# Rows of dt and of dt times x, spread for two scan units at a time, in a two-layer decoder with a selective scan

## The reference, cut to what matters

```
dt = softplus(dt_lowrank @ W_dt + b_dt)          # (256 tokens, 512 channels)
dA = exp(dt[..., None] * A)                      # 16 states for each channel
dBx = dt[..., None] * B_t[:, None, :] * x_t[..., None]
h = dA * h + dBx                                 # over the tokens
y_t = sum(h * C_t[:, None, :], axis=-1)
```

## Time and profile before

| what | value |
|---|---|
| time, median of 3 runs | 3942.16 us (3936.2 to 3948.75) |
| the profiled execution | 3951.12 us, span 3949.3 us |
| granted TensorE clock, mean | 0.933 |
| PE, DVE, ACT, POOL busy | 81%, 76%, 49%, 16% |
| DMA queue q1 | 205,552 packets, 467.17 MB, 39.2% of sixteen engines |
| one sequence | 232.8 us |

### The profile page before, as it was taken

The page is one execution under the profiler, slowest core; times in us unless marked ns, Lnnn a source line. Parts: engine busy times, 40 slices in busy tenths (PEclk is TensorE's granted clock), DMA queues, the critical chain, the costliest instruction groups (busy, mean ns, idle before and its releaser), DMA issues.

```text
span 3949.3 us, 57618 instructions
## 1 busy us (share of the span) xinstructions
PE 3210.4 (81%) x21250; PEld 2199.1 (56%) x21250; DVE 3004.6 (76%) x6496; ACT 1953.3 (49%) x4513; POOL 650.5 (16%) x516
## 2 busy tenths in 40 slices
PE   2468988788797888978888897988879888887877
PEld 1245656556464655646556564655646565564655
DVE  5678796877878688796868879687887868778632
ACT  2336455564545546455554645555464554645422
POOL 0303030120303012040210304021030301204000
PEclk8679999999999989999999999989999998999987
DMA  6526171532716235181523517153361614427100
GB/s 213 131 56 174 50 197 63 157 119 89 203 50 184 77 123 153 54 238 49 155 95 116 171 50 225 52 159 99 96 196 50 197 63 146 130 74 215 55 31 16
DMA packets 205833, 470.84 MB, mean 119 GB/s; under 512 B 23856, under 2 KB 43952, under 8 KB 190832
## 3 DMA queue, kind: packets, MB, share of 16 engines
q1 hardware_dynamic: 205552, 467.17, 39.2%
HBM read 446.11 MB, written 20.97 MB: 118 GB/s over the span
## 4 chain that ended last, share of the span: by engine, by line
PE 41%; DVE 34%; ACT 9%; issue 8%; DMA 6%; SPq 1%; POOL 0%; DVEq 0%; ACTq 0%
DVE region_x L1449 7%; PE ps L864 6%; DMA region_x<-rows_of_dt 5%; DVE region_x L1432 5%; PE ps L633 4%; PE ps L824 3%; PE ps L810 3%; PE ps L497 3%; ACT region_y L1148 3%; PE ps L845 3%; PE ps L614 2%; DVE nm L1486 2%; PE ps L645 2%; DVE x_stats L1284 2%; PE ps L569 2%
## 5 line engine op out<-in xcount | busy, mean ns | idle before, releaser
L1227 POOL TENSOR_TENSOR region_x<-region_x 128x512 f32<-128x512 f32 x512 | 650.3, 1270 | 2982.6 <-DVE region_x L1449 2982.6
L1028 ACT ACTIVATE ps<-region_x,aneg 128x255 f32<-128x255 f32 x1024 | 443.1, 470 | 446.2 <-DVE region_x L1449 431.3
L1449 DVE TENSOR_TENSOR_SCAN region_x<-ps,region_x 128x512 f32<-128x512 f32 x512 | 622.9, 1217 | 16.0 <-ACT ps L1028 15.1
L1432 DVE TENSOR_TENSOR region_x<-region_x,ps 128x512 f32<-128x512 f32 x512 | 343.1, 671 | 49.2 <-DMA region_x<-rows_of_dt 46.2
L864 PE MATMUL ps<-xTy,wide 128*128 128x256 f32 x1280 | 307.1, 395 | 0.0
L1148 ACT ACTIVATE region_y<-ps,rmax 128x256 f32<-128x256 f32 x512 | 235.7, 500 | 140.9 <-DVE rmax L1591 140.9
L1499 DVE SCALAR_TENSOR_TENSOR region_x<-region_x,cntk 128x512 f32<-128x512 f32 x256 | 167.0, 689 | 156.2 <-ACT region_x L1066 156.2
L864 PEld LDWEIGHTS ps<-xTy,wide 128*128 128x128 f32 x1280 | 244.5, 196 | 42.3 <-issue 10.1
L561 PE MATMUL ps<-region_x,sely 128*32 128x512 f32 x1024 | 157.5, 691 | 121.6 <-POOL region_x L1227 121.3
L614 PE MATMUL ps<-region_y 64*128 64x256 f32 x1024 | 176.9, 485 | 91.5 <-DVE VP L1572 37.4
L633 PE MATMUL ps<-region_y 64*128 64x256 f32 x1024 | 173.1, 464 | 95.9 <-ACT region_y L1066 49.5
(11 more groups left out here) (246 smaller groups left out, 6491.9 us busy)
## 6 DMA issues: line engine op xcount, KB each, us to landing
region_x<-rows_of_dt SPq DMA_DIRECT2D x1024, 256.0 KB, 5.3
wide<-in_wgate SPq DMA_DIRECT2D x16, 1280.0 KB, 8.4
wide<-in_wup SPq DMA_DIRECT2D x16, 1280.0 KB, 11.0
down<-in_wmoe SPq DMA_DIRECT2D x16, 1280.0 KB, 5.6
wide<-in_wq SPq DMA_DIRECT2D x16, 1024.0 KB, 4.8
wide<-in_wk SPq DMA_DIRECT2D x16, 1024.0 KB, 6.9
wide<-in_wv SPq DMA_DIRECT2D x16, 1024.0 KB, 8.9
down<-in_wo SPq DMA_DIRECT2D x16, 1024.0 KB, 7.8
```

The lines of the kernel that those rows point to most:

```text
L1028: last = f(ps[:, 1 + 2 * (k % 2), m * T + 1:(m + 1) * T], dt_rep[k % SLOTS][:, m, 1:T], ACT.Exp, scale=aneg[:, k, m:m + 1])
L1227: nc.gpsimd.tensor_tensor(hbuf[k % HSLOTS], hbuf[k % HSLOTS], csb.unsqueeze(1).to_broadcast([P, 2, T]), ALU.mult).then_inc(hc_ready, 1)
L1432: tt_(hbuf[k % HSLOTS], dtx_rep[k % SLOTS], ps[:, 2, 0:T].unsqueeze(1).to_broadcast([P, 2, T]), ALU.mult).then_inc(dbx, 1)
L1449: nc.vector.tensor_tensor_scan(flat(hbuf[k % HSLOTS]), ps[:, 1 + 2 * (k % 2), :], flat(hbuf[k % HSLOTS]), 0.0, ALU.mult, ALU.add).then_inc ...
```

## The change

Two neighbouring units are a couple. The scratch is laid out anew, `(parity, what, half, 32 rows r, 4 blocks j, 512)`, so that the rows of the two units of a couple are neighbours in DRAM. One spread then moves 8 rows of 4,096 bytes to 128 partitions, 512 KB, where two spreads of 8 rows of 2,048 bytes stood. Four slots of one unit become three slots of a couple (six units). A couple's dt waits for the decays of the whole couple three before it, its dt x for that couple's products. ACT and DVE wait for the couple's semaphore in both of its units.

The stores write the new layout: their DRAM side is `rearrange("r j f -> j r f")`, 4 x 32 rows of 512 values, with 128 partitions of 512 values on the SBUF side. The second stores stand behind the spreads of couple 1, which is the same place (four units).

The extra buffers lie in 2,048 more words of `region_x`; room for them comes from `dynamic_dma_scratch_size=1024`. Some semaphores that were never used are no longer made. `ORDER` is new for all engines.

```diff
-SLOTS = 4
+COUPLES = 3
 ORDER = {
-    "sp": (139, "x2 y3 x1 y1 x17 y1 x5 y1 x46"),
...
+    "sp": (63, "x13 y3 x2 y1 x14 y1 x2 y1 x8"),
...
-        dt_rep = [in_x(7436 + 512 * s, (2, T)) for s in range(SLOTS)]
-        dtx_rep = [in_x(9484 + 512 * s, (2, T)) for s in range(SLOTS)]
+        dt_rep = [in_x(at_word, (2, 2, T)) for at_word in (7436, 8460, 11792)]
+        dtx_rep = [in_x(at_word, (2, 2, T)) for at_word in (9484, 10508, 11792 + 1024)]
...
-        scratch = nc.dram_tensor("rows_of_dt", (2, 2, P, M * T), F32)
+        scratch = nc.dram_tensor("rows_of_dt", (2, 2, 2, 32, 4, 2 * T), F32)
...
+        def couple(i, d):
+            n = i * (UNITS // 2) + d
+            return n % COUPLES, 16 * (n // COUPLES + 1)
...
             def store_rows(i, what, src, half):
-                rows = scratch[i % 2, what][:, 512 * half:512 * half + 512]
+                rows = scratch[i % 2, what, half].rearrange("r j f -> j r f")
                 return sp.dma_start(rows, src[:, 2 * half:2 * half + 2].rearrange("p m t -> p (m t)"))

-            def spread_rows(i, what, k, dst):
-                pair, s, j = k // 16, k % 16 // 4, k % 4
-                first = 32 * j + 8 * s
-                rows = scratch[i % 2, what][first:first + 8, 512 * pair:512 * pair + 512]
-                return sp.dma_start(dst.rearrange("p m t -> p (m t)"), rows.unsqueeze(0).to_broadcast([NS, 8, 512]))
+            def spread_rows(i, what, d, dst):
+                rows = scratch[i % 2, what, d // 8, 8 * (d % 8 // 2):8 * (d % 8 // 2) + 8, 2 * (d % 2):2 * (d % 2) + 2]
+                return sp.dma_start(dst.rearrange("p k m t -> p (k m t)"),
+                                    rows.rearrange("r j f -> r (j f)").unsqueeze(0).to_broadcast([NS, 8, 4 * T]))
...
-                    if k == SLOTS:
+                    if d == COUPLES - 1:
                         yield from store_half(1)
...
-                    if k >= SLOTS:
-                        sp.wait_ge(decay_ready, at(i, UNITS, k - SLOTS + 1))
-                    spread_rows(i, 0, k, dt_rep[k % SLOTS]).then_inc(rep_dt[k % SLOTS], 16)
+                    if d >= COUPLES:
+                        sp.wait_ge(decay_ready, at(i, UNITS, 2 * (d - COUPLES) + 2))
+                    spread_rows(i, 0, d, dt_rep[slot]).then_inc(rep_dt[slot], 16)
...
-                    act.wait_ge(rep_dt[k % SLOTS], at(i, 128, 16 * (k // SLOTS + 1)))
+                    slot, landed = couple(i, k // 2)
+                    act.wait_ge(rep_dt[slot], landed)
...
-                    v.wait_ge(rep_dtx[k % SLOTS], at(i, 128, 16 * (k // SLOTS + 1)))
+                    slot, landed = couple(i, k // 2)
+                    v.wait_ge(rep_dtx[slot], landed)
```

More of the change, by code:

```diff
@@ L167, in build @@
         hmq = sb("hmq", (P, 4))
-        RX, RY = 11792, 9216
+        RX, RY = 13840, 9216
         region_x = sb("region_x", (P, RX))
@@ L245, in build @@
             sem("dt_ps"), sem("dt_x"), sem("dt_ln"), sem("dt_done"), sem("dtx_done"), [sem("dt_stored"), sem("dtx_stored")])
-        rep_dt = [sem(f"rep_dt{s}") for s in range(SLOTS)]
-        rep_dtx = [sem(f"rep_dtx{s}") for s in range(SLOTS)]
+        rep_dt = [sem(f"rep_dt{s}") for s in range(COUPLES)]
+        rep_dtx = [sem(f"rep_dtx{s}") for s in range(COUPLES)]
         pads, decay_ready, dbx, h_ready, hc_ready, y_ps, y_done = (
@@ L283, in __init__ @@
                     self.rinv = sb(tag + "_rinv", (P, TT, 4, 4))
+                    self.oT_ps, self.norm = sem(tag + "_oT_ps"), sem(tag + "_norm")
+                    self.on_ps, self.oT = sem(tag + "_on_ps"), sem(tag + "_oT")
+                else:
+                    self.kevac, self.rsum = sem(tag + "_kevac"), sem(tag + "_rsum")
+                    self.ln, self.shift = sem(tag + "_ln"), sem(tag + "_shift")
+                if masked:
+                    self.weighed = sem(tag + "_weighed")
                 self.proj = sem(tag + "_proj")
@@ L361, in first_half @@
                 yield from store_half(0)
-                for k in range(UNITS):
-                    if k:
+                for d in range(UNITS // 2):
+                    slot = couple(i, d)[0]
+                    if d:
                         yield
-                    if k == SLOTS:
+                    if d == COUPLES - 1:
                         yield from store_half(1)
-                    if k == 0 or k == UNITS // 2:
-                        sp.wait_ge(dt_stored[0], at(i, 32, 16 if k == 0 else 32))
-                    if k >= SLOTS:
-                        sp.wait_ge(decay_ready, at(i, UNITS, k - SLOTS + 1))
-                    spread_rows(i, 0, k, dt_rep[k % SLOTS]).then_inc(rep_dt[k % SLOTS], 16)
-                    yield
-                    if k >= SLOTS:
-                        sp.wait_ge(dbx, at(i, UNITS, k - SLOTS + 1))
-                    if k == 0 or k == UNITS // 2:
-                        sp.wait_ge(dt_stored[1], at(i, 32, 16 if k == 0 else 32))
-                    spread_rows(i, 1, k, dtx_rep[k % SLOTS]).then_inc(rep_dtx[k % SLOTS], 16)
-                    if k == 12:
+                    if d == 0 or d == 8:
+                        sp.wait_ge(dt_stored[0], at(i, 32, 16 if d == 0 else 32))
+                    if d >= COUPLES:
+                        sp.wait_ge(decay_ready, at(i, UNITS, 2 * (d - COUPLES) + 2))
+                    spread_rows(i, 0, d, dt_rep[slot]).then_inc(rep_dt[slot], 16)
+                    yield
+                    if d >= COUPLES:
+                        sp.wait_ge(dbx, at(i, UNITS, 2 * (d - COUPLES) + 2))
+                    if d == 0 or d == 8:
+                        sp.wait_ge(dt_stored[1], at(i, 32, 16 if d == 0 else 32))
+                    spread_rows(i, 1, d, dtx_rep[slot]).then_inc(rep_dtx[slot], 16)
+                    if d == 6:
                         yield
@@ L1027, in mamba @@
                     for m in range(2):
-                        last = f(ps[:, 1 + 2 * (k % 2), m * T + 1:(m + 1) * T], dt_rep[k % SLOTS][:, m, 1:T], ACT.Exp,
+                        last = f(ps[:, 1 + 2 * (k % 2), m * T + 1:(m + 1) * T], dt_rep[slot][:, k % 2, m, 1:T], ACT.Exp,
                                  scale=aneg[:, k, m:m + 1])
```

13 lines of the change are left out of this document (2 added, 11 removed), and 13 rows, old and new, of the table ORDER.

## The result

The changed kernel takes 4141.9 us (median of 4 runs, 4141.1 to 4147.5) against 3945.5 us for the kernel before on the same chip: ratio 1.0502, 95% interval 1.0476 to 1.0528. It is slower by 196 us, 12.3 us for each of the 16 sequences. The forecast was 3921 us, and the range up to 3968 does not hold the result.

The account below looks back on a forecast made before the run. The prediction took the kernel as bound by DVE in the scan and by PE after it. Ring -40, start +34 and order -15 gave -21 us, applied to the median of 3942.2: 3921 us, range 3880 to 3968 for 8 in 10.

Parts of the forecast that it names:

- Ring (-40): Spreads during the scan: longer lead ends most of DVE's 45.6 us of ring waits, -40 us off the span.
- The 180 ns: Time assumed for a 4,096-byte spread packet, between bounds of 158 and 258 ns; a couple then takes 2.9 us.
- Start (+34): Start of the scan: stores on four engines land later, 2.0 us in each of 15 sequences, some 4 in the first.
- Step 1: Start of the scan: the dt store takes 2.0 us more, first spread at 1680.4 instead of 1678.33; harmless by itself.
- Steps 2 and 3: Start of the scan: dt x store queues on the same engines, the first couple's dtx lands at 1686.5; loss 1.05 us.
- Step 4: Start of the scan: product 3 waits for the second half's stores, landed at 1694.5; loss 0.9 us a sequence.
- Order (-15): New order of engine pieces: wins 1 us a sequence, -15 us, with -30 to +15 as ends.
- B: Start of the scan: stores stay on sixteen engines or their lateness is hidden; 3884 us, chance 0.20.
- C: Time freed in the scan is absorbed, with PE full afterwards; 3942 us within 12, chance 0.18.
- D: Slower: a 4,096-byte spread packet costs 258 ns, start +61 us, order worth nothing or bad; 3963 to 3978 us, chance 0.22.
- Share at a quarter: Sign of being right: first stores move the same bytes at about a quarter of the sixteen-engine share.
- Products 0 and 3 waiting 1 to 2 us each: Sign of being right: at the scan's start these two products wait for DMA, 1 to 2 us each, in every sequence.

Follow-up runs that it names:

- d2: Ring of three couples with the old order, scratch and stores; each couple spread as two DMAs of 2,048-byte packets: ratio 0.9988 to the kernel before.
- g1: d2 with each of the four row stores cut into four DMAs of 32 partitions: ratio 1.0048 to the kernel before.
- d1: Changed kernel with the old PE, ACT and DVE order and each store cut into four DMAs; 4,096-byte packets, ring of three couples: ratio 1.0168 to before.
- a3: Changed kernel with the old order of PE, ACT and DVE: ratio 1.0359 to the kernel before.
- a1: Kernel before with only the scratch in the new layout, stores walked 4 x 32 x 512; spreads, slots and order as before: ratio 1.0396.
- a4: Kernel before with the new order of PE, ACT and DVE, all else as before: ratio 1.0188.
- c1: d1 with every spread reading 128 different 4,096-byte rows of a constant input, so the values spread are not the real ones: ratio 0.9969 to before.
- i2: Kernel before with every spread reading 128 different 2,048-byte rows of a constant input, so the values spread are not the real ones: ratio 0.9936.
- b2: Kernel before with six slots of one unit instead of four; packets, stores and order are the old ones: ratio 0.9951.
- h1: a1 with only the second half's two stores on four engines; the first half's are cut into four DMAs: ratio 1.0274 to the kernel before.
- a2: Changed kernel with each store cut into four DMAs of 32 partitions, so on sixteen engines: ratio 1.0335 to the kernel before.
- f3: Kernel before with ACT's guess2 and guess3 moved behind the experts' first and second gates, adding two table loads a sequence: ratio 1.0167.
- i1: a2 with guess2 and guess3 moved back ahead in ACT's order alone, two table loads fewer a sequence: ratio 1.0535 to the kernel before.
- f2: Kernel before with the new order up to the end of the latent attention and the old order from there: ratio 1.0334.
- j1: Kernel before, order untouched, with one more table change at the end of an ACT piece, two table loads more a sequence: ratio 0.9993.

## Why the prediction was wrong

The runs make a ladder from before to after, each step one difference (in us of 3945):

| step | runs | us |
|---|---|---|
| ring of three couples, 2,048-byte packets | d2 | -5 |
| stores as four DMAs each | g1 - d2 | +24 |
| 4,096-byte spread packets | d1 - g1 | +47 |
| stores as one DMA on four engines | a3 - d1 | +75 |
| new order | after - a3 | +56 |

Together +197. By the intervals the differences are good to 8 to 13 us, the first to 4. The change has no stores cut in four; the second and the fourth step together are the way from the old stores to the new, +99 us. The parts do not simply add: alone on the kernel before, the stores cost 156 us (a1) and the order 74 (a4).

**Ring (-40).** Products 4 to 31 wait 40 us more (76.1 against 36.0), where the forecast took 40 off. Two steps failed.

The first is the packet. The 180 ns were taken as nearest to twice the quiet packet of the earlier trace rows; the changed kernel shows 263, past its upper bound of 258. The quiet stretch was misread. Its packets are hardly spreads: the second half's two stores land between 1688.19 and 1690.60, and their 256 packets fill most of 1687.8 to 1689.2. The first spreads, with no other transfer beside them, already take more:

```profile
1679.10:1684.00 4.90, 3.76 (x21) 2.91 (x19) 3.02 (x7) 3.11 (x7) 0.00 (x0) 1.00 0.76 208
```

That is 0.76 x 32768 / 208 = 120 ns, and two crowded packets of the earlier trace rows take 258. And the bytes do not set the packet alone: against different rows of an input, reading eight rows of the scratch sixteen times costs 78 ns of 274 and 23 of 125 (c1, i2). At 263 ns a couple fills 16 x 0.263 = 4.2 us of every engine and the spreads of 32 units 67 us of the 80 the scan has, and the landing became longer (median 7.9 us, before 5.3).

The second is the lead. The forecast counted 8.6 us ahead for a couple instead of 6.8 and let the waits go with it. d2 has this ring with the old packets, and products 4 to 31 wait as long as before (36.1 us). A couple is asked for only when both units of the one three before are through, and used only when both of its own have landed; b2 asks and waits for single units, and there the waits are gone. With c1's faster packets the ring of couples is enough (2.1 us). That waits come off the span one for one was wrong too: b2 took 38 us of waits away and 19 of time; 10.5 went to waits for ACT's decays, and where the rest went is open.

The forecast cited the Trainium skill, Perfetto Trace Analysis, DMA Optimizations, by which batching 2 KB transfers into 4 KB ones can improve throughput dramatically. The runs disagree for this spread: g1 with 2,048-byte packets is 47 us faster than d1. Even where all rows are different there is little in it: two 2,048-byte packets take 204 ns in i2, one of 4,096 takes 196 in c1.

**Start (+34).** The mechanism was right, the size was not: products 0 and 1 wait 106 us more than before and products 2 and 3 another 22.5; a1 measures +156 us for the stores alone, the ladder +99 in the changed kernel. That the stores would use four engines was seen, in the share of 0.25 and the four landings.

By the Trainium skill, DMA: Bandwidth & Descriptors ("Why a DMA increments its semaphore by 16 and not by 1"), the number of engines is the largest up to 16 that divides the slowest dimension of both sides. The trace agrees, with its share of 0.25.

Step 1 had the first spread 4.1 us after the store; it came 6.19 us after. Of the 2.1 us between, some 1.5 are the slow first packets (the first store's packets last 4.3 us in all), 0.4 that the first packet starts later (1.21 us after the issue, before 0.83), and 0.3 lie between the last packet and the issue of the spread. Steps 2 and 3 had both stores landed after 6.8 us and the first couple's dtx 3.4 us behind that, 10.2 in all; measured are 8.9 and 5.3, and product 0 starts at 14.24. Step 4, product 3's gate, was near: 0.9 us forecast, 12.8 + 6.1 us over 14 sequences measured. It is larger, 44 us in all, where the second stores wait behind 2,048-byte spreads (h1).

Not all of the start is the stores. With all stores on sixteen engines a2 still waits 71.3 us at products 0 and 1: cutting them costs some (g1), the large packets some (d1 against g1: 49.3 against 41.9), and the new order some (a2 against d1).

**Order (-15).** Wrong in sign: +74 us alone (a4), +56 in the changed kernel, outside the bounds of -30 to +15. The forecast priced it by the waits the moves aim at, and a4 shows those waits longer. Landmarks on PE put a4's loss of 5.4 us in one sequence at 1.5 ahead of the router (L854, in a4 L850), 3.5 from there to the experts' last matmuls (L925, in a4 L921) and 0.4 behind. Part of it is clock: the eight matmuls of the latent attention's output projection (L671), which now stand right behind the router, ran in that sequence (1862.5 to 1866) at a granted clock of 0.52, nearly all at 1.2 GHz, after PE had been busy 2.70 of 4 us; over the span this group is busy 42.3 us instead of 31.9. Which moves cause the rest stays open: f3 and i1 say what two pieces of ACT cost when they are moved alone, f2 that the two halves of the order do not add up, and j1 that the added table loads are not it.

**Rivals.** B fell with the share of 0.25. C did not occur. D named the packet (258 ns, measured 263) and the side, and was still 164 us short at its far end, since it kept the ring's -40, had the start at +61 and let the order cost at most 15 us.

**Signs named beforehand.** Share at a quarter: seen. Products 0 and 3 waiting 1 to 2 us each: product 0 waits 5 us and more in every sequence (7.49 in the one shown), product 3 waits 0.2 to 2.1 us in 14 of 16. Hardly any later product waiting and packets near 180 ns: not seen; the product line waited in mid-scan, which the forecast had named as the sign that the lead time was not mended.

## What to carry to other kernels

Before fewer and larger DMAs are counted as a gain, multiply the new packet by its count from a stretch as crowded as the one it will run in, and compare it with the time the consumer leaves; with a source read many times over, try it. Check whose packets a stretch holds before taking a packet's time from it: the landings tell. Look at both sides of a small store that now has a short outermost dimension, and at everything that waits for its landing: here the first spreads and, behind a queue of spreads, product 3. And lead time can be bought by itself: two more slots for single units gave 19 us with nothing else touched, where six slots in couples left the waits as they were.

## What the runs showed that was not expected

A packet that reads eight rows of the scratch, each read 16 times, is slower than one that reads 128 different rows of an input: 274 ns against 196 at 4,096 bytes (d1, c1), 125 against 102 at 2,048 (before, i2), at the same 234 to 241 GB/s. Whether it is the sharing or the tensor was not parted.

A store on four engines starts slowly: its packets take 85 ns like those on sixteen, but about twenty of the first take 0.1 to 1 us each, and the first store's packets last 4.3 us instead of 0.83.

A transfer on sixteen engines that is queued behind such a store lands in two groups: twelve parts, and 4 to 6 us later the four that share its engines (h1).

Late data also went with a lower TensorE clock. Five microseconds of h1 with 0.87 us of work on PE, and the two stretches behind them:

```profile
1725.00:1730.00 5.00, 0.87 (x8) 0.42 (x6) 3.04 (x5) 1.61 (x4) 0.00 (x0) 0.67 0.97 261
1730.00:1735.00 5.00, 4.49 (x24) 3.24 (x24) 4.09 (x5) 1.74 (x4) 2.53 (x2) 0.64 1.01 295
1735.00:1740.00 5.00, 1.48 (x10) 1.02 (x8) 3.07 (x4) 0.02 (x1) 0.04 (x1) 0.70 0.99 278
```

And the same place in the kernel before:

```profile
1684.00:1689.00 5.00, 1.41 (x10) 0.97 (x12) 4.13 (x9) 2.31 (x6) 0.00 (x0) 0.75 1.03 305
1689.00:1694.00 5.00, 4.82 (x24) 3.15 (x24) 5.00 (x6) 1.74 (x4) 2.53 (x2) 0.57 0.98 324
1694.00:1699.00 5.00, 3.51 (x26) 2.06 (x24) 4.89 (x6) 0.87 (x2) 1.26 (x1) 1.00 1.02 323
```

Both dip to a mix of the two levels, 2.4 and 1.2 GHz, but the kernel before is back at 2.4 GHz in the third stretch and h1, idle again, is not. Over the span the granted clock is 0.933 before and 0.911 after, and PE's busy time for the same matmuls rose from 3210.4 to 3267.4 us; in b2 it is 0.936 and 3203.4 us.
